# Start of a perceiver block: keys, values, transposes, then queries as three rounded products, with loads in halves

## What is computed

```python
x = x + xattn(layernorm(x), ctx, Wq, bq, Wk, bk, Wv, bv, Wo, bo)   # 16 heads of 32
    # q = ln(x) @ Wq.T + bq ; k = ctx @ Wk.T + bk ; v = ctx @ Wv.T + bv
    # s = q k^T / sqrt(32) ; p = where(s >= 0, s + 1, 1 / (1 - s)) ; p /= sum(p)
    # out = (p v) @ Wo.T + bo
x = x + attn(layernorm(x), ...)       # causal self-attention, 8 query heads, one key/value head
x = x + ffn(layernorm(x), ...)        # 2 shared experts and 8 routed ones, top 2, hidden 2048
```

## Time and profile before

| | |
|---|---|
| time, median of 3 runs | 1272.35 us (1272.26 to 1272.46) |
| the profiled execution: its own time | 1272.52 us |
| its span | 1270.8 us |
| TensorE busy | 1260.8 us, 99% |
| VectorE, ScalarE, GpSimd busy | 51%, 50%, 34% |

### The profile page before, as it was taken

How to read it: one execution, slowest core, us unless ns; L and a number is a source line. 1 busy time by engine, 2 the same in 40 slices (tenths; PEclk the granted TensorE clock), 3 DMA queues, 4 the chain that set the end, 5 groups by cost and what they waited for, 6 DMA issues and landing times.

```text
span 1270.8 us, 29915 instructions
## 1 busy us (share of the span) xinstructions
PE 1260.8 (99%) x13126; PEld 1097.3 (86%) x13126; DVE 649.4 (51%) x936; ACT 634.2 (50%) x1085; POOL 437.4 (34%) x203
## 2 busy tenths in 40 slices
PE   9999999999999999999999999999999999999998
PEld 8888888888788888888789789798989999999997
DVE  5333453444463363463354454766776555565655
ACT  4445454464545544545444646646544443554443
POOL 1445345544555545545546535200032000100000
PEclk9999999999999999999999999999999999999999
DMA  6131011021011012012012111764556499999990
GB/s 244 50 103 51 18 56 50 23 68 67 19 64 68 18 56 101 19 64 68 18 51 105 51 56 43 284 255 157 179 195 224 148 348 365 340 344 347 357 396 35
DMA packets 32775, 174.89 MB, mean 138 GB/s; under 512 B 5944, under 2 KB 8152, under 8 KB 14464
## 3 DMA queue, kind: packets, MB, share of 16 engines
q1 hardware_dynamic: 30896, 168.16, 36.0%
q0 software_dynamic: 1744, 4.76, 1.2%
HBM read 166.84 MB, written 6.06 MB: 136 GB/s over the span
## 4 chain that ended last, share of the span: by engine, by line
PE 98%; DVE 1%; DMA 0%; ACT 0%; issue 0%; DVEq 0%; SPq 0%
PE bank L740 23%; PE bank L728 22%; PE bank L1079 11%; PE sc L1096 9%; PE sc L756 8%; PE sc L941 7%; PE bank L769 4%; PE sc L960 3%; PE bank L960 3%; PE bank L833 1%; PE bank L796 1%; PE bank L887 1%; PE bank L898 1%; PE sc L898 1%; DMA ctxt<-in_ctx 0%; PE sc L999 0%
## 5 line engine op out<-in xcount | busy, mean ns | idle before, releaser
L587 POOL TENSOR_TENSOR xn<-xn,tt 128x1024 f32<-128x1024 f32 x96 | 230.1, 2397 | 330.9 <-DVE tt L1325 329.7
L1208 ACT ACTIVATE tt<-sc 128x512 f32<-128x512 f32 (+1 forms) x208 | 107.8, 602 | 351.5 <-PE sc L756 351.4
L1423 DVE TENSOR_TENSOR wsl<-ring,wsh 128x2048 fp32r<-128x2048 f32 x72 | 166.8, 2316 | 111.0 <-ACT wsh L1163 107.9
L1312 DVE TENSOR_SCALAR kk<-bank,bkt 128x512 f32<-128x512 f32 (+2 forms) x130 | 80.8, 622 | 213.6 <-PE bank L728 213.2
L728 PE MATMUL bank<-cxh,wkh 128*128 128x512 f32 (+2 forms) x512 | 181.1, 354 | 1.5 <-DVE va L1320 1.0
L728 PE MATMUL bank<-cxl,wkh 128*128 128x512 f32 (+2 forms) x512 | 174.6, 341 | 0.0
L728 PE MATMUL bank<-cxh,wkl 128*128 128x512 f32 (+2 forms) x512 | 174.1, 340 | 0.0
L740 PE MATMUL bank<-wvh,cxh 128*128 128x512 f32 (+1 forms) x416 | 163.5, 393 | 0.0
L740 PE MATMUL bank<-wvl,cxh 128*128 128x512 f32 (+1 forms) x416 | 162.7, 391 | 0.0
L740 PE MATMUL bank<-wvh,cxl 128*128 128x512 f32 (+1 forms) x416 | 162.2, 390 | 0.0
L1163 ACT CAST wsh<-ring 128x2048 fp32r<-128x2048 f32 x72 | 137.4, 1909 | 48.0 <-PE sc L1096 20.9
(11 more groups left out here) (270 smaller groups left out, 2024.2 us busy)
## 6 DMA issues: line engine op xcount, KB each, us to landing
ring<-in_w SPq DMA_DIRECT2D x112, 1024.0 KB, 6.1
ctxt<-in_ctx SPq DMA_DIRECT2D x15, 1024.0 KB, 4.9
ctxt<-in_ctx SPq DMA_DIRECT2D x8, 642.0 KB, 3.9
ctxt<-in_ctx SPq DMA_DIRECT2D x10, 512.0 KB, 3.6
wqt<-in_wo SPq DMA_DIRECT2D x4, 1024.0 KB, 4.8
wqt<-in_aq SPq DMA_DIRECT2D x4, 1024.0 KB, 5.3
wqt<-in_ap_ SPq DMA_DIRECT2D x4, 1024.0 KB, 6.9
yrows<-K SPq DMA_DIRECT2D x1, 2048.0 KB, 9.1
```

Source lines behind the costliest of these rows:

```text
L587: e.tensor_tensor(dacc[0:kn, y, :], dacc[0:kn, y, :], tt[0:kn, w, :], ALU.add).then_inc(s["da_pool"], 1)
L1423: e.tensor_tensor(wsl[m % 3][:], ring[slot(unit_split(m))][:], wsh[m % 3][:].bitcast(F32), ALU.subtract).then_inc(s["wl_dve"], 1)
```

## The change

- Loads: all of wk, wv, x and wq come in two halves of 512 KB, each with a semaphore of its own, in the order wk, context part 0 (behind wk's first half), wv, x, wq. Context part 1 goes to the second half of ctxt, which is free, right behind them and ahead of the small loads, with no wait.
- Order on TensorE: first keys (now c by c, with three products for each c), `values(0)`, `turn(0)`, `turn(1)`, `values(1)`, `turn(2)`, `turn(3)`, queries, and then the scores. `turn(t)` for t = 2, 3 waits for `turned_lo(t - 2)` on VectorE.
- The first keys go to banks 4 to 7, so that the first projections need not wait for banks 0 and 1.
- Queries are three products, woh with xTh, woh with xTl and wol with xTh. woh and wol, free at this time, hold the parts of Wq. g = 0 and 1 go in two steps of 256 rows, g = 2 and 3 in one of 512.
- ScalarE rounds wv's halves ahead of the roots, then wq's halves with `root(0, 2)` and `root(0, 3)` between and behind, and writes the high part of every turned tile (`turned_hi`).
- VectorE makes wvl in halves ahead of the statistics, which start when a half of x is there, and behind the four keys it reads values and writes the low part of every turned tile (`turned_lo`, PSUM minus xTh).
- GpSimd makes the low part of wq in halves (`query_weights_lo`), ahead of `context_lo(1)`.

The core of the diff:

```diff
-            e.dma_start(wkt[:, 0:2, :], wk[:, 0:2, :]).then_inc(s["wk_in"], 16)
-            load_ctx(0)
-            e.dma_start(wkt[:, 2:4, :], wk[:, 2:4, :]).then_inc(s["wk2_in"], 16)
+            for h in range(2):
+                e.dma_start(wkt[:, 2 * h:2 * h + 2, :], wk[:, 2 * h:2 * h + 2, :]).then_inc(wk_in[h], 16)
+                if h == 0:
+                    e.dma_start(ctxt[:, 0:1024], ctx0[0, :, 0:1024]).then_inc(s["c0_in"], 16)
             e.dma_start(bkt[:], bk).then_inc(s["bk_in"], 16)
-            e.dma_start(xres[:], x).then_inc(s["x_in"], 16)
-            e.dma_start(wqt[:], wq).then_inc(s["wq_in"], 16)
-            e.dma_start(wvt[:], wv).then_inc(s["wv_in"], 16)
+            for src, dst, landed in ((wv, wvt, wv_in), (x, xres, x_in), (wq, wqt, wq_in)):
+                for h in range(2):
+                    c = slice(2 * h, 2 * h + 2)
+                    e.dma_start(dst[:, c, :], src[:, c, :]).then_inc(landed[h], 16)
+            e.dma_start(ctxt[:, 1024:2048], ctx0[0, :, 1024:2048]).then_inc(s["ctx_in"], 16)
...
+            def query_weights_lo(h):
+                c = slice(2 * h, 2 * h + 2)
+                e.wait_ge(s["wqh_act"], h + 1)
+                e.tensor_tensor(wol[:, c, :], wqt[:, c, :], woh[:, c, :].bitcast(F32),
+                                ALU.subtract).then_inc(s["wql_pool"], 1)
+
             e.memset(K2[:], 0.0).then_inc(s["k2_pool"], 1)
+            for h in range(2):
+                query_weights_lo(h)
             context_lo(1)
...
             def turn(t, dst):
                 e.wait_ge(s["xn_dve"], t + 1)
+                if t >= 2:
+                    e.wait_ge(s["xt_dve"], t - 1)
...
-            def queries(g, h):
-
-                for c in range(4):
-                    m = e.matmul(bank[QUERY[g]][:, 256 * h:256 * h + 256], wqt[:, c, g * P:(g + 1) * P],
-                                 xT[:, c, 256 * h:256 * h + 256], start=(c == 0), stop=(c == 3))
-                if h:
+            def queries(g, tiles):
+
+                cols = slice(P * tiles[0], P * tiles[-1] + P)
+                for x_, (w_, x__) in enumerate(((woh, xTh), (woh, xTl), (wol, xTh))):
+                    if (g, tiles[0]) == (0, 0) and x_ == 0:
+                        e.wait_ge(s["wqh_act"], 2)
+                    for c in range(4):
+                        if (g, tiles[0]) == (0, 0) and x_ == 2 and c % 2 == 0:
+                            e.wait_ge(s["wql_pool"], c // 2 + 1)
+                        m = e.matmul(bank[QUERY[g]][:, cols], w_[:, c, g * P:(g + 1) * P], x__[:, c, cols],
+                                     start=(x_ == 0 and c == 0), stop=(x_ == 2 and c == 3))
+                if tiles[-1] == 3:
                     m.then_inc(s["q_pe"], 1)
 
+            values(0)
             for t in range(2):
                 turn(t, bank[2 + t])
-            e.wait_ge(s["wq_in"], 16)
-            e.wait_ge(s["xt_act"], 2)
-            for g in range(2):
-                queries(g, 0)
+            values(1)
             for t in range(2, 4):
                 turn(t, bank[t])
             e.wait_ge(s["proj_read"], use["k", 0, 3] + 1)
+            e.wait_ge(s["xt_dve"], 2)
+            for g in range(2):
+                queries(g, (0, 1))
+            e.wait_ge(s["xt_dve"], 4)
+            for g in range(2):
+                queries(g, (2, 3))
             for g in range(2, 4):
-                queries(g, 0)
-            e.wait_ge(s["xt_act"], 3)
-            e.wait_ge(s["xt_dve"], 1)
-            for g in range(4):
-                queries(g, 1)
-            for n in range(2):
-                values(n)
+                queries(g, (0, 1, 2, 3))
...
@@ act, behind the roundings of wk, context part 0 and wv
             for t in range(2):
                 root(0, t)
+            for h in range(2):
+                c = slice(2 * h, 2 * h + 2)
+                e.wait_ge(wq_in[h], 16)
+                e.copy(woh[:, c, :], wqt[:, c, :]).then_inc(s["wqh_act"], 1)
+                root(0, 2 + h)
             for t in range(2):
-                turned(t, bank[2 + t])
+                turned_hi(t, bank[2 + t])
+            context_hi(1)
             for t in range(2, 4):
-                root(0, t)
-            turned(2, bank[2])
-            e.wait_ge(s["wv_in"], 16)
-            e.copy(wvh[:], wvt[:]).then_inc(s["wvh_act"], 1)
-            context_hi(1)
+                turned_hi(t, bank[t])
...
@@ vector, behind wkl and the low part of context part 0
+            for h in range(2):
+                c = slice(2 * h, 2 * h + 2)
+                e.wait_ge(s["wvh_act"], h + 1)
+                e.tensor_tensor(wvl[:, c, :], wvt[:, c, :], wvh[:, c, :].bitcast(F32),
+                                ALU.subtract).then_inc(s["wvl_dve"], 1)
+            e.wait_ge(x_in[0], 16)
+            for t in range(2):
+                stats_of(0, t)
+            for t in range(2):
+                rows(0, t)
+            e.wait_ge(x_in[1], 16)
+            for t in range(2, 4):
+                stats_of(0, t)
+            for t in range(2, 4):
+                rows(0, t)
             for g in range(4):
                 keys(0, g)
-            turned(3, bank[3])
-            e.wait_ge(s["wvh_act"], 1)
-            e.tensor_tensor(wvl[:], wvt[:], wvh[:].bitcast(F32), ALU.subtract).then_inc(s["wvl_dve"], 1)
+            values(0)
+            for t in range(2):
+                turned_lo(t, bank[2 + t])
+            values(1)
+            for t in range(2, 4):
+                turned_lo(t, bank[t])
```

More of the change, by code:

```diff
@@ L197, in build @@
         with ExitStack() as over:
+            xTh = over.enter_context(nc.sbuf_tensor("xTh", [P, 4, D], F32R))
+        with ExitStack() as over:
             xT = over.enter_context(nc.sbuf_tensor("xT", [P, 4, D], F32))
@@ L281, in build @@
         qc = sb1("qc", [P, 4, D])
+        with ExitStack() as over:
+            over.enter_context(nc.sbuf_tensor("tt01", [P, 2, 1024], F32))
+            xTl = over.enter_context(nc.sbuf_tensor("xTl", [P, 4, D], F32R))
         tt = sb1("tt", [P, TR, 1024])
@@ L692, in take @@
                 u = use[what]
-                if u >= 2:
+                if u >= 6:
                     e.wait_ge(s["proj_read"], u - 1)
@@ L699, in first_keys @@
                 n = width(0)
-                for h in range(2):
+                for c in range(4):
                     for x_, (a, b) in enumerate(((0, 0), (1, 0), (0, 1))):
[L702 to L710, removed]
-                        for g in range(4):
[L712 to L716, removed]
+                        if x_ == 0 and c % 2 == 0:
+                            e.wait_ge(s["wkh_act"], c // 2 + 1)
+                            e.wait_ge(s["c0_act"], 1)
+                        elif x_ == 1 and c % 2 == 0:
+                            e.wait_ge(s["wkl_dve"], c // 2 + 1)
+                        elif x_ == 2 and c == 0:
+                            e.wait_ge(s["c0_dve"], 1)
+                        for g in range(4):
+                            m = e.matmul(key_bank(0, g)[:, 0:n], (wkh, wkl)[a][:, c, g * P:(g + 1) * P],
+                                         (cxh, cxl)[b][:, 0, c, 0:n], start=(x_ == 0 and c == 0),
+                                         stop=(x_ == 2 and c == 3))
+                            if (c, x_) == (3, 2):
                                 m.then_inc(s["k_pe"], 1)
@@ L735, in values @@
                 dst = take("v", n)
-                if n == 0:
-                    e.wait_ge(s["wvl_dve"], 1)
                 for c in range(4):
+                    if n == 0 and c % 2 == 0:
+                        e.wait_ge(s["wvl_dve"], c // 2 + 1)
                     for x_, (a, b) in enumerate(three):
@@ L1337, in rows, with turned_lo @@
                                 ALU.subtract, ALU.mult).then_inc(s["xa_dve" if l else "xn_dve"], 1)
[L1339 to L1342, removed]
+            def turned_lo(t, src):
+                e.wait_ge(s["xth_act"], t + 1)
+                e.tensor_tensor(xTl[:, :, t * P:(t + 1) * P], src[:].rearrange("p (c k) -> p c k", c=4),
+                                xTh[:, :, t * P:(t + 1) * P].bitcast(F32), ALU.subtract).then_inc(s["xt_dve"], 1)
             def rows_turned(t):
@@ L1473, in vector @@
             e.memset(epsb[:], EPS).then_inc(s["eps_dve"], 1)
[L1474 to L1477, removed]
-                                wkh[:, 2 * c:2 * c + 2, :].bitcast(F32), ALU.subtract).then_inc(s["wkl_dve"], 1)
-                if c == 0:
-                    e.wait_ge(s["ch_act"], 1)
-                    e.tensor_tensor(lo, src, hi.bitcast(F32), ALU.subtract).then_inc(s["cl_dve"], 1)
@@ L1482, in vector @@
-            e.wait_ge(s["x_in"], 16)
-            for h in range(2):
-                for t in range(2 * h, 2 * h + 2):
-                    stats_of(0, t)
-                for t in range(2 * h, 2 * h + 2):
-                    rows(0, t)
+            for h in range(2):
+                c = slice(2 * h, 2 * h + 2)
```

(9 more changed lines are left out.)

52 lines of the change are left out of this document (30 added, 22 removed).

## The result

| | median us | lowest to highest | runs |
|---|---|---|---|
| before | 1272.39 | 1272.26 to 1272.52 | 6 |
| changed | 1277.41 | 1276.51 to 1277.56 | 6 |

The changed kernel takes 1.0038 times as long, 95% interval 1.0025 to 1.0051: slower by 5.0 us, where 4.7 us were forecast. Its profiled execution has a span of 1275.8 us and a time of 1277.49 us.

A forecast was written before the change was run, and what follows sets the result against it. TensorE, busy 99% of the span, was taken as the bound: first scores 2.3 us later plus 2.4 us for a lower clock, 4.7 us in all, gave 1277.1 us from the median. Range 1273.3 to 1279.9 us.

The forecast's parts named there:

- TensorE's work: Queries: 13.8 us of plain float32 matmuls replaced by 11.2 us of three-product ones, 2.6 us less.
- The tail: Between queries and first scores: TensorE waits for ScalarE's last query write, 1.15 us exposed.
- The loads: At the start: wv's halves land at 9.3 and 10.6 us, wq's first at 14.5 to 15.2 us.
- a late wq: Allowance at the scores if wq's load lands late: up to 0.9 us more, beside the 2.3 us shift.
- the likeliest case: Whole kernel: rows held once each and the clock falls, 1277.1 us, chance 0.62.
- The hold: VectorE's rows(0,2) and rows(0,3) wait out GpSimd's two wq subtractions, ending at 19.0 and 21.5 us.
- The wait at turn(2): TensorE idles 4.4 us after values(1), until VectorE's turned_lo(0) ends at 24.3 us.
- The clock: TensorE's granted clock falls to 1.2 GHz through the idle stretch, costing 2.4 us (1.5 to 3.4 us).
- (a): Clock stays up through TensorE's idle stretch: +2.3 to +3.2 us, 1274.7 to 1275.6 us, chance 0.10.
- (b): VectorE's rows(0,t) are not held by GpSimd: 1272.6 to 1275.0 us, chance 0.14.
- (c): GpSimd starts its next operation past the waiting VectorE, TensorE idle 7 us: 1279.8 us, chance 0.10.

The follow-up runs named there:

- e5: e3 with the queries as plain float32 matmuls, as before the change; only TensorE's work differs: 1273.78 us.
- e3: Changed kernel with turned_lo of tiles 0 and 1 ahead of rows(0,2) on VectorE, their turned_hi and both roots ahead of wq's second half on ScalarE: 1271.17 us.
- e1: Changed kernel with GpSimd waiting for the fourth normalised tile before it subtracts wq's low half: 1274.01 us.
- e6: Changed kernel with GpSimd's subtraction of wq in four quarters instead of two halves: 1274.60 us.
- e2: Changed kernel with 85 matmuls on constants filling TensorE's idle stretch before turn(2), first keys packed two to a bank: 1275.40 us.
- e4: e3 with first keys packed two to a bank, queries not waiting for key reads, third products later, and scores waiting g by g: 1270.09 us.
- e7: e4 with turned_lo of tiles 2 and 3 ahead of the two value reads on VectorE: 1269.23 us.

## Why the prediction was right

The total, 1277.4 against 1277.1 us, is closer than its terms. By its own steps:

- **TensorE's work, 2.6 us less.** Right. e5 against e3 is 2.6 us in the medians and 2.5 us in the chains; the forecast's own terms, 13.8 less 5.8 and 5.5 us, give 2.5 us too.
- **The tail, 1.15 us.** Right, a little large: the wait row shows 0.8 us, counted from the modelled end of the last matmul. The queries' slots end about 0.2 us before that (24 of 0.23 us from 34.18 us on), so it was 1.0 us.
- **The loads.** Mis-sized: wv's second half was taken by ScalarE at 10.97 us (10.6 forecast), and wq's first half at 16.02 us, where 15.2 us was forecast; ScalarE's row of wqh shows 0.56 us of waiting for the load. The first wql therefore started at 17.15 instead of 16.3 us, and everything behind it is 0.85 us late. That is the 0.9 us that stood beside the sum for a late wq: the likeliest case had left it out, and it came.
- **The hold.** Right in kind, place and length: rows(0,2) ended 0.3 us behind GpSimd's first operation, GpSimd's waiting one went next, and rows(0,3) ended 0.3 us behind the second. e1 shows the cause, e6 the handover, for which the rows of before had no case with a second GpSimd operation ready. The rule of the Trainium skill ("SBUF — State Buffer", Who interferes with whom), by which rows(0,2) goes ahead of the second wql, agrees with the trace: rows(0,2) had stood ready since 17.57 us and ends near 19.8 us, and GpSimd's second operation ends only at 22.05 us. Its record begins at 19.52 us, ahead of that, but is 2.53 us long instead of 2.40 us, so part of it is waiting.
- **The wait at turn(2).** 4.4 us forecast, 5.1 us measured, the difference being the late wq. Hold and order share it: without the hold (e1) 2.5 us are left, and with turned_lo ahead of the rows and GpSimd's second operation behind them (e3) nothing.
- **The clock.** Fell, as forecast. 2.4 us were set and 2.1 us measured by e2. The term was worked out from 4.9 us at the lower level at the start; here it was 5.1 us, but 1.9 us of that were the transposes, which take 1.22 us at the full clock (e2) and so lost only 0.7 us; the second four of them also wait for turned_lo(1). That the clock would fall was right with a margin that was not known: at the end of the old kernel it fell some 2 us behind the last matmul, here some 3.4 us behind it, of 5.1 us idle.

Summed with these terms in place of the forecast's: 2.3 + 0.85 - 0.15 + 2.1 = 5.1 us, against 5.15 us at the scores and 5.0 us in the total. The late load (+0.85) and the smaller tail and clock (-0.45) partly cancelled, and that the total came within 0.3 us is luck to that extent. Of the rivals, (a) came true in no run of the changed kernel; in e1 and e6, whose idle stretches are 2.5 and 3.2 us, one run in ten each is as fast as it would be with the clock up (mean clock 1.000). (b) fell with the two rows' 4.76 us, and e1 shows why; (c) fell with the two turns, in the changed kernel and in e6. What stays open is why the changed kernel's one run of 1276.51 us was 0.9 us below the others; runs that weren't profiled have no windows, and its mean clock (0.998 against 0.997) only suggests a shorter time at the lower level.

## What to carry to other kernels

When a stage is moved onto GpSimd, list VectorE's operations that will stand beside it and sort them by their operands: in this kernel those with two inputs in SBUF, and tensor_scalar from SBUF to SBUF, waited to the end of GpSimd's operation, while those with a PSUM input ran at full pace, and so did a BATCH_NORM_AGGREGATE from SBUF (0.18 us at 17.48 us, beside GpSimd). Then put the latter where GpSimd is busy, and cut GpSimd's operations short where the former can't move. And work out every order by what TensorE waits for next: work taken off TensorE (2.6 us here) is worth nothing while it idles, and an idle stretch can be paid for again by the clock (5.1 us idle cost a further 2.1 us here).

## What the runs showed of the hardware

- Two engines that hold each other up take turns, operation by operation, in both directions (17.15 to 22.33 us in the changed kernel, 17.28 to 20.3 us in e6).
- The granted clock can fall where TensorE is not idle: in e3 in the window 36 to 37 us, at the end of 64 matmuls of 32 x 64 that follow a wait of 0.8 us. In e1 it fell in the window 23 to 24 us (0.62) and in e6 in the window 24 to 25 us (0.89), when TensorE had been at work again since 22.43 and 23.20 us, behind 2.5 and 3.2 us of idle time. An idle stretch can thus be over before its price is due.
- The fall cost the profiled run of e3 1.5 us; one more of its ten runs, and one of ten of e2, are longer by as much. With the wait before the scores hidden (e4, e7), none of twenty runs was over 0.35 us above the lowest of its kernel. That this wait is the cause is likely, not shown.
- With an idle stretch of 2.5 us (e1) the same program gave three separate times, 1272.4, 1273.9 and 1275.5 us. Where the chain holds no idle time at all (e7) it gave one, within 0.31 us.
